# A second wait ahead of a group of gathers in a recommendation kernel

## The reference

```
dense_emb  = relu(relu(dense @ dw1 + db1) @ dw2 + db2)        # 2048 x 64
sparse_emb = emb_tables[f, sparse_idx[:, f]]                   # 2048 x 26 x 64
emb   = concat([dense_emb, sparse_emb])                        # 2048 x 27 x 64
inter = einsum('bfd,bgd->bfg', emb, emb)                       # gram of each sample
pairs = inter[:, upper triangle]                               # 2048 x 351
z = concat([emb.reshape(2048, 1728), pairs])
y = relu(relu(relu(z @ ow1 + ob1) @ ow2 + ob2) @ ow3 + ob3) @ ow4 + ob4
```

## Time and profile before

| | |
|---|---|
| plain runs, median of 3 | 543.22 us (543.18 to 543.4) |
| profiled execution, first to last instruction | 704.8 us |
| POOL busy | 392.8 us, 56% of the span |
| PE busy | 484.0 us, 69% |
| DVE busy | 151.4 us, 21% |
| ACT busy | 148.4 us, 21% |
| mean granted TensorE clock | 0.818 |

### The profile page before, as it was taken

The page is one execution under the profiler, slowest core; times in us unless marked ns, Lnnn a source line. Parts: engine busy times, 40 slices in busy tenths (PEclk is TensorE's granted clock), DMA queues, the critical chain, the costliest instruction groups (busy, mean ns, idle before and its releaser), DMA issues.

```text
span 704.8 us, 5797 instructions
## 1 busy us (share of the span) xinstructions
PE 484.0 (69%) x2262; PEld 265.8 (38%) x2262; DVE 151.4 (21%) x295; ACT 148.4 (21%) x334; POOL 392.8 (56%) x420
## 2 busy tenths in 40 slices
PE   4864928659286693938759487693937938597788
PEld 1223414334143342424334243342414423254666
DVE  1021302122030221402222030320402213131223
ACT  2312203121111312203122121212203122121312
POOL 6756464764647466564764647466464665647330
PEclk9986967959589596977959789596976979779799
DMA  8522231221313222131221213223231231322110
GB/s 250 98 20 23 19 23 15 26 22 17 22 15 26 20 19 23 18 23 16 24 23 17 22 16 26 20 19 22 18 24 16 21 22 18 22 18 26 12 14 2
DMA packets 17167, 19.39 MB, mean 28 GB/s; under 512 B 7359, under 2 KB 8386, under 8 KB 17127
## 3 DMA queue, kind: packets, MB, share of 16 engines
q0 software_dynamic: 13312, 13.66, 23.2%
q1 hardware_dynamic: 3408, 5.02, 2.1%
q10 hardware_dynamic: 420, 0.34, 0.2%
HBM read 18.99 MB, written 0.01 MB: 27 GB/s over the span
## 4 chain that ended last, share of the span: by engine, by line
another core or an unknown queue 42%; PE 34%; DVE 11%; issue 9%; ACT 4%; DMA 0%; DVEq 0%
PE l_ps L678 9%; PE gram_ps L657 8%; PE l_ps L686 8%; DVE slots L291 4%; DVE gram_c L315 2%; PE l_ps L669 2%; PE tr_ps L640 1%; DVE feat L282 1%; DVE pairs L296 1%; PE l_ps L772 1%; PE tr_ps L621 1%; DVE h1t L303 1%; ACT slots L443 1%; ACT gram_c L455 1%
## 5 line engine op out<-in xcount | busy, mean ns | idle before, releaser
L247 POOL DMA_INDIRECT emb<-table_dram,rows x416 | 392.6, 944 | 287.1 <-issue 117.0
L678 PE MATMUL l_ps<-w_sb,feat 128*128 128x512 f32 x390 | 197.9, 656 | 13.9 <-DVE feat L282 7.2
L657 PE MATMUL gram_ps<-slots 64*128 64x108 f32 x960 | 88.8, 352 | 144.1 <-DVE gram_c L315 139.5
L657 PEld LDWEIGHTS gram_ps<-slots 64*128 64x128 f32 x960 | 81.6, 258 | 161.7 <-DVE gram_c L315 145.0
L678 PEld LDWEIGHTS l_ps<-w_sb,feat 128*128 128x128 f32 x390 | 77.6, 209 | 120.8 <-issue 110.5
L315 DVE COPY gram_c<-gram_ps 32x432 f32<-32x432 f32 x60 | 36.5, 609 | 343.4 <-remote 275.5
L455 ACT COPY gram_c<-gram_ps 32x432 f32<-32x432 f32 x60 | 30.5, 508 | 305.5 <-remote 262.8
L686 PE MATMUL l_ps<-w1p_sb,pairs 118*128 118x512 f32 x90 | 53.4, 740 | 14.4 <-DVE pairs L296 11.9
L621 PE MATMUL tr_ps<-ident_sb,emb 128*128 128x128 f32 x203 | 36.6, 291 | 23.9 <-DMA emb<-table_dram,rows 13.5
L443 ACT COPY slots<-tr_ps 64x256 f32<-64x256 f32 (+1 forms) x128 | 50.3, 393 | 1.1
L621 PEld LDWEIGHTS tr_ps<-ident_sb,emb 128*128 128x128 f32 x203 | 26.6, 149 | 53.8 <-issue 35.9
(11 more groups left out here) (103 smaller groups left out, 202.9 us busy)
## 6 DMA issues: line engine op xcount, KB each, us to landing
emb<-table_dram,rows POOLq DMA_INDIRECT x416
w_sb<-ow_dram SPq DMA_DIRECT2D x3, 1024.0 KB, 7.4
w1p_sb<-ow_pairs_dram SPq DMA_DIRECT2D x1, 708.0 KB
w_sb<-ow_dram SPq DMA_DIRECT2D x1, 512.0 KB
w_sb<-ow_dram SPq DMA_DIRECT2D x1, 256.0 KB
idx_raw<-idx_dram ACTq DMA_DIRECT2D x1, 208.0 KB, 2.7
w1d_sb<-ow_dram SPq DMA_DIRECT2D x1, 128.0 KB
w_sb<-ow_dram SPq DMA_DIRECT2D x1, 128.0 KB
```

Source lines behind the costliest of these rows:

```text
L247: pool.indirect_dma_start(out=emb[:, t % RING, c // 2, c % 2 * D:(c % 2 + 1) * D], out_offset=None, in_=table, in_offset=bass.IndirectOffs ...
L657: mm = nc.tensor.matmul(gram_ps[:, bank, r * GCOLS:(r + 1) * GCOLS], x.rearrange("p c f -> p (c f)"), x[:, :, 0:SLOTS], start=True, stop=True)
L678: nc.tensor.matmul(l1_ps[t % 2][:], feat[t % 2][:, n - 1, :], w1_sb[:, n - 1, :], start=False, stop=False)
```

## The change

One wait is added to POOL's queue in each of the tiles 1 to 15. Group 1 of tile t, which already waits for the transposes of group 3 of tile t-1, now also waits until `gram_done` has reached 2t - 1, which is the end of `gram(t-1, 0)`. On PE that gram half comes after the transposes of group 3 and features 9 to 13 of the same tile.

```diff
                 for n, (a, b) in enumerate(GROUPS):
                     if t >= 1:
                         pool.wait_ge(transposed, t * NG + (-2, 0, 1, 2)[n])
+                        if n == 1:
+                            pool.wait_ge(gram_done, 2 * t - 1)
                     for c in range(2 * a, 2 * b):
                         pool.indirect_dma_start(
```

## The result

The changed kernel takes 564.89 us (median of 4; 564.59 to 566.25) against 543.28 us (543.18 to 543.4): a ratio of 1.0401, 95% interval 1.0389 to 1.0414. It is 21.6 us slower. Forecast were 563.5 us and a range of 543.0 to 580.0.

What follows compares the result with a forecast made beforehand. POOL's unbroken issue of gathers, 32.44 us per tile, was taken as the bound of plain runs. The wait was to add 14 x 1.45 = 20.3 us to 543.2, giving 563.5 us, with a range of 543.0 to 580.

Steps and rivals of the forecast that it cites:

- The ring: Way from one gram event through POOL, DMA and PE to the next: 32.14 us at full clock, 33.80 with lost clock.
- loss by the clock: PE's features and gram slow down after idle gaps: 1.66 us a tile, up to 4.1 after a long idle.
- the 1.66 of the pair matmuls: Pair matmuls at half clock took 4.50 us against 2.84 in the tile before; taken as the loss per tile.
- POOL's pace: POOL issuing 26 gathers a tile at 1.2475 us each without a break: 32.44 us per tile.
- The count and the price: POOL's added waits: 14 tiles paying 1.45 us each, 20.3 us; tile 1's wait falls in the setup and is left out.
- PE's idle: PE waits 3.4 us ahead of group 2 and 1.9 ahead of group 3, 5.3 us of slack a tile.
- The bound: POOL's issue of 416 gathers, back to back, sets the plain run's time; their starts span up to 521.8 us.
- the hold: PE's semaphore updates kept back until gathers drain; taken to belong to the profiled execution, most of its extra 161.6 us.
- The term for the end: Time from the start of POOL's last gather to the end of the profile: 25.7 us, unchanged by the change.
- the sum of 547.5: Back-to-back gathers, 521.8 us, plus 25.7 at the end: 0.8% above the plain median.
- "faster" rival: Late PE updates partly real in plain runs, the wait lets them through: at most 1.4 us a tile, 523 us; chance 0.08.
- What the changed profile would show: Eleventh gather waits for the gram, PE's 11 us idle shrinks as POOL pauses, clock 0.50 in features, span falls.

Runs made afterwards that it cites:

- The extra gather: Kernel before the change plus one more gather of 128 rows ahead of group 0 in tiles 1 to 15: 732.73 us against 715.36, ratio 1.0257.
- experiment 9: Gram halves of tiles 0 to 14 replaced by four matmuls each: 668.9 to 697.8 us without the added wait, 772.27 with it; kernel before 711.48.
- the filling: Four dummy matmuls ahead of group 2's wait, tiles 1 to 12: changed kernel 1.041 and 1.045 of the kernel before; without the added wait 0.9988.
- experiment 4: Changed kernel with the added wait eight gathers earlier, ahead of group 0: 946.39 us against 715.36 for the kernel before, ratio 1.324.
- experiment 3: Changed kernel with the added wait eight gathers later, ahead of group 2: 690.53 us against 707.25 for the kernel before, ratio 0.9795.

## Why the prediction was right, and where its reasons were not

**The ring.** The mechanism is the one forecast: gram event, 18 gathers, landing, transpose, features, gram. Its terms outside the 21.2 us of gathers, from the profile after and as forecast:

| term | forecast | measured |
|---|---|---|
| last gather to its transpose | 3.34 | 3.43 (239.04 to 242.47) |
| transpose to features | 0.33 | 0.24 (to 242.71) |
| features to gram, at full clock | 4.49 | 4.38 in tile 14 (515.38 to 519.76) |
| loss by the clock | 1.75 | 2.03 (242.71 to 249.12 is 6.41) |
| gram and its event | 2.49 | 2.06 (249.12 to 251.18, by the chain) |
| event to POOL's gather | 0.28 | 0.76 (to 251.94) |

(The loss of 1.75 is the 1.66 of the pair matmuls with the rounding up to 1.45 us over POOL's pace.) The right column sums to 12.90, the left to 12.68; with the gathers the ring is 34.1 us, against 33.9. At full clock the right column would be 10.87 and the ring 21.21 + 10.87 = 32.08 us, as forecast: 0.36 under POOL's pace. The loss by the clock was taken a little small, from a stretch of 3.3 us at 1.2 GHz; it was 4.0.

**The count and the price.** Fourteen tiles were to pay 1.45 us each, 20.3 in all. Tiles 2 to 14 paid, thirteen; tile 1 paid 0.14, and tile 15, which I had left in, nothing, because the gram half that it waits for came at full clock. The trace gives the price: the 12 waits of the row are 23.5 us, less twelve gaps of 0.30 is 19.9; the thirteenth adds 2.32 - 0.30 = 2.0: 21.9 us, 1.68 a tile. The times say 21.6. The count was one too high and the price 0.23 us too low, and the two errors offset each other in part (1.45 us too much, 13 x 0.23 = 3.0 too little). That the sum came within 1.4 us of the measured 564.89 is partly luck.

**PE's idle.** Laid out as 3.4 and 1.9 us; measured 4.93 and 1.43. The rows named for the layout make the end of the pair matmuls 25.5 rather than 25.0 (20.8 + 1.84 + 2.84), and the first idle 2.9. The prediction said that PE's gap does not shrink when POOL is held, and it does not. Nor does the clock need a held POOL to fall: tile 1, in front of which POOL lost only 0.14 us, has idles of 2.50 and 1.76 us and features of 6.52 us. Tile 13 lost its clock with 1.83 us of idle, and tile 14, left in the count, did not.

**The bound.** That POOL issues without a break at 543 us has no profile of its own. The profile after supports it: POOL has no idle there but the usual gaps, the gram and the start, and the 21.9 us of pauses are the whole difference in time. The extra gather agrees, at 1.16 us each, but under the hold. The term for the end was wrong: 25.7 us behind the last gather in the profile before, 19.1 (563.4 - 544.3) after. With 19.1, and the 1.8 us around the span, the sum of 547.5 becomes 542.7. In the "faster" rival 32.8 stands in no row; with POOL's 32.44 the gain would be at most 1.0 us a tile.

**The hold.** "The hold belongs to the profiled execution" is wrong as put. Every run on the four chips of the experiments has its long times, and the profile of 563.4 us has no trace of it. What the changed profile would show came true in two points, the eleventh gather that waits for the gram and the clock of 0.50 in the features. In the third it erred: PE's idle of 11 us is gone because this execution has no hold at all, and not because POOL pauses. The forecast was right since the condition of the times, 543 us, was rightly read as one without hold. What sets the condition, the chip or something else, stays open. A third fewer matmul records do not lift it (experiment 9). In the earlier trace rows the update of a gram that ended 12 us into an unbroken run of gathers came only 4 us after the start of the last one; the profile after has unbroken runs of 26 gathers, 32 us, without any hold.

**What is shown and what is argued.** Shown, in one execution: POOL waits about 1.7 us for the gram in thirteen tiles, each time behind features that ran in part at half clock, and hardly or not at all in the two tiles where they ran at full clock. Those two tiles, the first and the last before tile 15, differ from the rest in other work too; the filling that was to repeat the case in the middle ran under the hold and can't decide it. Not shown is whether PE loses its clock at the same place in the kernel before at 543 us, of which there is no profile. That the place sets the price is shown under the hold (experiment 4 costs 231 us, experiment 3 nothing).

## What to carry to other kernels

An added wait on the engine that sets the pace costs nothing only as long as the whole ring through it, gathers, landing and all that PE does ahead of the event, is shorter than the pace. Sum the ring with the clock that PE will have there: here it was the half one behind idles of 4.9 and 1.4 us and also, in one tile, behind a single idle of 1.8 us, but not where the idles were 0.8 and 1.4. And compare the profile's span with the times first; where they differ by a third, the profile is of another condition, and only its durations can be carried over.

## What the runs showed of the hardware

One kernel took 543 us in one set of runs and 701 to 721 us on four chips, run after run, with the same 0.944 us for a gather and the same 3.3 us to landing; the difference shows as a delay of up to 13.5 us (303.44 to 316.94 in the earlier trace rows) between PE's work and the arrival of its semaphore updates while gathers are being issued. Under it a wait in every second tile gained 4.6%, where in the other condition a wait in every tile lost 4.0%.

TensorE's granted clock fell to 1.2 GHz in the features of thirteen tiles, in one of them behind a longest idle of 1.83 us and 3.7 us of work ahead of the transposes, and stayed there for 3 to 4 us.
